# GpSimd fills the padding rows of batches 1 to 3, batch 1 is split in three pieces, batch 0's values are projected earlier

## What is computed

```python
q, k, v = heads(xn @ Wq + bq), heads(xn @ Wk + bk), heads(xn @ Wv + bv)      # xn = layernorm(x), 16 heads of 8
y  = softmax(causal(q @ k.T * scale)) @ v
qc, kc, vc = heads(xn @ Wcq + bcq), heads(ctx @ Wck + bck), heads(ctx @ Wcv + bcv)
y += softmax(qc @ kc.T * scale) @ vc
x = x + tanh(g_xattn[0]) * (y @ Wp + bp)
x = x + tanh(g_ffn[0]) * moe0(layernorm(x))      # top 2 of 8 experts, with a capacity
x = x + tanh(g_xattn[1]) * attention1(layernorm(x), ctx)      # one head
x = x + tanh(g_ffn[1]) * moe1(layernorm(x))      # top 2 of 8 experts
```

## Time and profile before

| | us |
|---|---|
| median of 3 runs | 383.36 (382.57 to 384.79) |
| the profiled execution: its own time | 384.66 |
| its span in the profile | 382.9 |
| busy PE, DVE, ACT, POOL | 331.7, 240.0, 188.9, 103.8 |
| mean granted TensorE clock | 0.957 of full speed |

### The profile page before, as it was taken

The page is one execution under the profiler, slowest core; times in us unless marked ns, Lnnn a source line. Parts: engine busy times, 40 slices in busy tenths (PEclk is TensorE's granted clock), DMA queues, the critical chain, the costliest instruction groups (busy, mean ns, idle before and its releaser), DMA issues.

```text
span 382.9 us, 6988 instructions
## 1 busy us (share of the span) xinstructions
PE 331.7 (87%) x2646; PEld 192.9 (50%) x2646; DVE 240.0 (63%) x566; ACT 188.9 (49%) x387; POOL 103.8 (27%) x173
## 2 busy tenths in 40 slices
PE   4879959988899998778979699999988499899994
PEld 2445624434343343333456467776775346575663
DVE  5787778888988888747545042233310958658765
ACT  3366237787778778667518622232217333324220
POOL 5526102125222322223276102223432201100000
PEclk9989968999999999999989879999999889999999
DMA  7779993121305002250061380000002100000100
GB/s 171 189 185 211 210 217 69 31 102 42 114 2 169 4 2 79 90 169 2 2 197 52 89 216 25 16 9 20 21 14 84 41 2 1 0 2 0 30 0 27
DMA packets 35635, 27.80 MB, mean 73 GB/s; under 512 B 5436, under 2 KB 32880, under 8 KB 35602
## 3 DMA queue, kind: packets, MB, share of 16 engines
q1 hardware_dynamic: 33718, 25.34, 26.4%
q0 software_dynamic: 1280, 1.88, 1.5%
q10 hardware_dynamic: 604, 0.14, 0.2%
HBM read 11.89 MB, written 5.26 MB: 45 GB/s over the span
## 4 chain that ended last, share of the span: by engine, by line
PE 70%; DVE 11%; ACT 6%; DMA 5%; issue 4%; POOL 2%; ACTq 1%; SPq 1%; POOLq 0%; DVEq 0%
PE psum L1433 11%; PE psum L1632 11%; PE psum L1663 7%; PE psum L1616 6%; PE psum L1651 4%; PE psum L1375 4%; PE psum L1399 4%; PE psum L1367 3%; PE psum L1451 2%; DVE nmax L1008 2%; PE psum L1311 2%; ACT ot_sb L787 2%; PE psum L1377 1%; PE psum L1564 1%; ACT qk L812 1%
## 5 line engine op out<-in xcount | busy, mean ns | idle before, releaser
L1008 DVE TENSOR_REDUCE nmax<-psum 128x2 f32<-128x1024 f32 (+2 forms) x88 | 104.5, 1216 | 21.2 <-PE psum L1375 12.8
L812 ACT ACTIVATE parts<-psum 128x512 f32<-128x512 f32 (+1 forms) x88 | 44.7, 569 | 12.9 <-PE psum L1399 12.3
L1151 DVE TENSOR_TENSOR qcat<-psum,qk_r 128x320 f32<-128x320 f32 x32 | 15.7, 491 | 45.9 <-ACT qk_r L853 45.8
L1632 PE MATMUL psum<-p_more,kcat 128*128 128x320 f32 x128 | 43.0, 478 | 0.7 <-DVE p_more L1142 0.7
L853 ACT ACTIVATE qk_r<-psum 128x320 f32<-128x320 f32 x32 | 14.0, 438 | 49.4 <-PE psum L1632 49.4
L709 POOL DMA_INDIRECT rows_back<-qcat,back_at x24 | 22.9, 954 | 56.1 <-ACT qcat L844 51.2
L1632 PEld LDWEIGHTS psum<-p_more,kcat 128*128 128x128 f32 x128 | 23.6, 202 | 14.4 <-issue 6.0
L1663 PE MATMUL psum<-h_t,kcat 128*128 128x512 f32 x64 | 30.1, 596 | 0.7 <-ACT h_t L823 0.7
L1375 PE MATMUL psum<-kcat,qcat 64*128 64x512 bf16 x128 | 25.9, 401 | 5.4 <-DVE nmax L1008 4.9
L1399 PE MATMUL psum<-qcat,kcat 64*128 64x256 bf16 x256 | 25.7, 280 | 3.4 <-ACT p_more L812 1.4
L1433 PE MATMUL psum<-parts,v_aug 128*9 128x256 f32 (+1 forms) x352 | 28.3, 366 | 0.0
(11 more groups left out here) (216 smaller groups left out, 605.4 us busy)
## 6 DMA issues: line engine op xcount, KB each, us to landing
kcat<-parts SPq DMA_DIRECT2D x18, 192.0 KB, 5.4
qcat<-parts SPq DMA_DIRECT2D x24, 128.0 KB, 4.8
kcat<-ones_b SPq DMA_DIRECT2D x8, 192.0 KB, 5.1
kcat<-in_L_ffn_wi_gate_dram SPq DMA_DIRECT2D x6, 256.0 KB, 3.2
kcat<-in_L_ffn_wi_up_dram SPq DMA_DIRECT2D x6, 256.0 KB, 4.0
kcat<-in_L_ffn_wo_dram SPq DMA_DIRECT2D x6, 256.0 KB, 4.5
parts<-in_L_ffn_w_dram SPq DMA_DIRECT2D x3, 512.0 KB, 5.6
rows_in<-zeros SPq DMA_DIRECT2D x1, 1290.0 KB, 6.0
```

The lines of the kernel that those rows point to most:

```text
L812: act.activation(p_slots[u % NPT][:, 0:w], s2_bank(s2_place[u])[:, 0:w], ACT.Exp, scale=SCALE).then_inc(p_in, 1)
L1008: dve.tensor_reduce(dst[:, :, n * g:n * (g + 1)], src.rearrange("p (r q k) -> p r q k", r=PAR, q=n), AX.X, ALU.max, negate=True).then_inc( ...
L1151: dve.tensor_tensor(hh[:, e % 2, f, 0:SLOTS], bank(3 + 2 * (i % 2))[:, 0:SLOTS], sg[:, i % 2, 0:SLOTS], ALU.mult).then_inc(hh_in[0], 1)
L1632: ins = pe.matmul(bank(2 + 2 * (i % 2) + m)[:, 0:SLOTS], w_t[e][:, m, f * P:(f + 1) * P], xs_t[:, e % 2, :], start=True, stop=True)
```

## The change

The padding rows of batches 1 to 3 are no longer written by DMA. GpSimd fills the whole `qcat` of a batch with zeros and the whole `kcat` with ones (as 32-bit words that hold two bf16 ones) in `fill(b)`, before the parts are laid out over them. `fill(1)` stands behind the last `rstd_group` of the first normalisation, `fill(2)` behind GpSimd's constants, and `fill(3)` behind its subtractions. VectorE splits batch 1 in three pieces as q, k and ck come. The jobs `v` and `cv` of batch 0 move ahead of `q`, `k` and `ck` of batch 3; `N_FIRST` stays.

```diff
         N_FIRST = len(jobs) - 5
-        for b in range(B):
+        jobs[-3:-3] = [("v", 0), ("cv", 0)]
+        for b in range(1, B):
             jobs += [("v", b), ("cv", b)]
...
+        TWO_ONES = 1.0 + 0x3F80 / 2.0 ** 23
+        def pad_count(b):
+            return 16 * 4 if b == 0 else 2
...
             def lay_out_batch(b):
+                sp.wait_ge(pad_in[b], pad_count(b))
                 sp.wait_ge(parts_in, b + 1)
...
-            pad(1)
             lay_out_batch(1)
-            pad(2)
-            pad(3)
             lay_out_batch(2)
...
+            def fill(b):
+                pool.memset(qcat[:, b].rearrange("p g c -> p (g c)").bitcast(F32), 0.0).then_inc(pad_in[b], 1)
+                pool.memset(kcat[:, b].rearrange("p g c -> p (g c)").bitcast(F32), TWO_ONES).then_inc(pad_in[b], 1)
+            fill(1)
             const(pool.tensor_copy(ident_b[:, :], ident[:, :]))
...
             const(pool.memset(v_aug[:, :, :, HD:HA], 1.0))
+            fill(2)
             for b in range(SPLIT_DVE, B):
...
+            fill(3)
...
             for b in range(1, SPLIT_DVE):
-                dve.wait_ge(job_act, taken_count(job_at("ck", b)))
-                split(b, 0, XW, True)
+                for job, first, end in (("q", 0, QW), ("k", QW, QW + S), ("ck", QW + S, XW)):
+                    dve.wait_ge(job_act, taken_count(job_at(job, b)))
+                    split(b, first, end, job == "ck")
```

More of the change, by code:

```diff
@@ L493, in _ @@
             sp.wait_ge(zero_in, 2)
-            pad(0)
+            for r in (M_ROW, M_ROW + 1):
+                sp.dma_start(every(kcat, 0, r), ones_b[:, :]).then_inc(pad_in[0], 16)
+                sp.dma_start(every(qcat, 0, r), zeros[:, 0:QW // 2].bitcast(BF16)).then_inc(pad_in[0], 16)
             sp.wait_ge(early_in, 1)
@@ L544, in _ @@
                     if n % 2 == 0 and par == 0:
-                        sp.wait_ge(pad_in[n // 2], 16 * 4)
+                        sp.wait_ge(pad_in[n // 2], pad_count(n // 2))
                     sp.dma_start(dst[:, PP * (n % 2):PP * (n % 2 + 1), :],
@@ L1358, in pass1_unit @@
                     pe.wait_ge(cat_in[b], 16 * 2 * NPROD)
-                    pe.wait_ge(pad_in[b], 16 * 4)
+                    pe.wait_ge(pad_in[b], pad_count(b))
                 if kind == "late" and part == 0:
```

## The result

| | before | after |
|---|---|---|
| median, both on the same chip | 384.08 us (382.57 to 390.33, 4 runs) | 394.32 us (393.3 to 398.75, 4 runs) |
| the profiled execution: time, span | 384.66, 382.9 | 393.66, 391.9 |
| busy PE, DVE, ACT, POOL | 331.7, 240.0, 188.9, 103.8 | 335.1, 252.2, 188.9, 117.3 |
| mean granted TensorE clock | 0.957 | 0.940 |

The change makes the kernel slower: ratio 1.0281, 95% interval 1.0242 to 1.0321, which is 10.8 us on 384. I had forecast 388.8 us and at most 392. The sign and the place were right, the size was not.

What follows compares the result with a forecast made beforehand. It took the start of pass 2, behind batch 1's split and the maxima's DMAs, to bound the kernel. Terms +6.0, +2.0 and -2.7, with VectorE at +5.9 partly catching up, gave +5.4 on 383.36: 388.8 us, range 382.5 to 392.

Steps and rivals of the forecast that it cites:

- The bound and the path: Start of pass 2 at 52.59 us: a shift there goes through to the end of the kernel.
- Part 1, the DMAs that go: SyncE's queue before pass 2: the maxima land 3.1 us after issue, not 5.8; -2.7 us, bounds -2.9 and 0.
- Parts 2 and 3, the split and the fills: VectorE before pass 1: pieces save 1.6 us, fills cost 7.6; together +6.0 us, bounds +4.5 and +7.4.
- Part 4: Moved jobs make fill(3) meet the two casts of split_max before pass 2: +2.0 us, range 0 to 3.5.
- unit 2 on TensorE, which then stands from 24.5 to 32: Pass 1: unit 2 queues behind VectorE's later first reduction, with TensorE standing from 24.5 to 32 us.
- Rival (a): Fills in the split hold nobody up, only parts 1 and 2 remain: 379.4 us, down to 378; chance 0.20.
- I put it at 0: ScalarE's split_middle(3) waits for GpSimd with v and cv of batch 1 behind it: cost taken as 0.
- The sum at P: First matmul of pass 2 on TensorE: start at 57.9 us against 52.59, +5.3.
- (b): Fills hold VectorE less and fill(3) misses split_max; pass 1 some 2.5 us late: 383 to 384.5 us; chance 0.11.
- (c): The maxima's landing before pass 2 stays 5.8 us: +8.1, 391.5 us; chance 0.07.

Runs made afterwards that it cites:

- e3: The changed kernel with fill(3) moved between GpSimd's two subtractions of batch 2; ratio 1.0131 to the kernel before.
- e9: The kernel of e7 with GpSimd also waiting for its own semaphore before fill(3) and between its two memsets; one time, 389.63 us.
- e14: The changed kernel with the jobs v and cv of batch 0 back in their old place; ratio 1.0076 to the kernel before.
- e7: The changed kernel with seven unused products of 128x512 f32 filling TensorE's gap before unit 2; ratio 1.0143 to the kernel before.
- e11: The kernel before with only the jobs v and cv of batch 0 moved; ratio 1.0004 to the kernel before.
- e4: The changed kernel with all three fills moved beside VectorE's reductions from PSUM; ratio 1.0039 to the kernel before.
- e10: The kernel before with only the split of batch 1 in pieces; ratio 1.0011 to the kernel before.
- e12: The kernel before with batch 1 split in pieces, pad(1) behind batch 1's layout, pads 2 and 3 behind the second maxima; ratio 0.9910 to the kernel before.
- e5: The changed kernel with each memset of the fills cut into eight pieces at the same places; ratio 1.0152 to the kernel before.
- e1: The changed kernel without its fills, padding by DMA as before, split in pieces and moved jobs kept; ratio 1.0004 to the kernel before.
- e2: The changed kernel with only the fills, batch 1 split in one piece and jobs in old order; ratio 1.0255 to the kernel before.

## Why the prediction missed

**The bound and the path: right.** A later start of pass 2 went through to the end (+9.67 at P, +10.5 at the last score matmul, +9.0 in the span). The other kernels of the table that start pass 2 later than before end it later by the same and 0.1 to 1.2 us more.

**Part 1, the DMAs that go: right as far as it can be seen.** Forecast 3.1 us from issue to landing and a gain of 2.7; measured 3.3 from issue to the first matmul and a gain of 2.6. But that matmul no longer waits for the DMA, so the landing itself is only known to be 3.3 us or less. VectorE, which I had at +5.9, is at +10.5 and sets the rest.

**Parts 2 and 3, the split and the fills: right in kind, 1.0 us too high.** The memsets took 1.80 to 2.07 and 2.65 to 2.80 us against my 1.8 and 2.65. The casts and `tensor_scalar` were held and the subtractions not, by the mechanism of the earlier trace rows. Forecast +6.0 for unit 2, measured +5.0. The Trainium skill, page "SBUF — State Buffer", section "Who interferes with whom", has the loser wait for a whole instruction of the other engine; the trace agrees for the long casts of the split, the longest 2.50 us under a memset of 2.80. For the cast at 50.94 its sentence is too mild: that one waited through what remained of one instruction and through two more, and the measurement decides.

**Part 4, "I take 2.0, as one `qcat` memset": failed.** It was 4.25 us, beyond my bound of 3.5. That bound took the rest of one memset for each of two casts. In fact the first cast met the subtraction L659 in front of `fill(3)` and was then let through at neither of the two ends of instructions (51.4 and 53.2), so it stood for all three. e3 takes 4.96 us off M by moving this one fill, and e9 shows that a pause of 0.06 us in GpSimd's work lets the casts through. That they meet was foreseen, and by the right path (`ck` of batch 3 behind the moved jobs): GpSimd's last subtraction moved 3.4 us against `split_max` (from e14 to after: ended 2.9 before it, now 0.5 behind its start), forecast 2.9.

**"What queues behind it: ... unit 2 on TensorE, which then stands from 24.5 to 32": this was where the sum lacked a term.** I saw the gap and priced what waited, but not the clock behind it. It stayed at 1.2 GHz until 41 us. Up to `split_max` that took 3.0 us more than the low clock of the kernel before takes there. e7 shows it: unit 2 at the same time, full clock, M 4.65 us earlier. After the next stop, while `split_max` was held, the low clock came again, from 55 to 68 us, but the kernel before has it too after its own stop, from 50 to 60. The profile had told me. Rival (a) of the prediction even counts a low clock of "some 3 us" after the gap of 1.67 us, as a gain if it goes. I used the row in one direction only.

**"I put it at 0", for ScalarE: no run speaks against it.** `split_middle(2)`, which I had not looked at, now stands behind the copies of the moved jobs and comes at 37.73, 4.7 us later than in e14. But GpSimd is done with the subtraction that needs it at 41.67 and then waits 3.16 us for `ck` of batch 3, and ScalarE itself waits 0.79 us for TensorE behind it. So that delay costs nothing here. What the moved jobs cost once the fills are there (by e14 7.9 us in the ratios, 5.2 in the span, and by e11 nothing without them) goes through the two terms above, the cast and the clock.

The sum at P: forecast 57.9, measured 62.26. The difference of 4.4 is -1.0 (parts 2 and 3), +3.0 (clock), +2.25 (part 4) and +0.1 (from the DMA to the matmul). The median went up by 10.2, or 10.8 by the ratio, against 9.0 for the span of the profiled execution: its clock of 0.940 was the highest of the four (another had 0.940 too, with 393.3; the others 0.937 with 394.97 and 0.911 with 398.75).

**The rivals.** (a), fills that hold nobody up, is out. e4 nearly is that kernel, and even it isn't faster. (b) and (c) are out too: all three fills met casts or `tensor_scalar`, and the landing fell to 3.3 us or less. The clock is in none of them as a loss.

**Still open.** Why the 32-column cast is passed over at the ends of GpSimd's back-to-back instructions, and the casts of batch 1 are not: in `fill(1)` and `fill(2)` three of four memsets took 0.15 us or more longer than in `fill(3)`, as if they had waited for a cast, and in `fill(3)` none did. And what sets how long the low clock lasts, 3.4 us in one kernel and 34 in another, and whether it comes at all: behind the gap of 1.13 us in e10 and e12 it did not. The length of the gap alone does not set it: in the profiled execution of e11 it is 37 us behind the same gap of 1.67 us that has 3.4 us in the kernel before.

## What to carry to other kernels

Before work is moved onto GpSimd, lay its instructions over VectorE's timeline and look at every cast, copy and `tensor_scalar` that they cover. Put the fill beside reductions from PSUM or subtractions, and count a train of back-to-back GpSimd instructions as one, as the worst case. Where a change makes TensorE stand, add to the gap what its following work costs at the lower clock, from rows of the same products at both levels. And where a small DMA lands late behind large ones, first try another order of SyncE's queue: here that, with the split in pieces, gave 3.5 us, and the change with its clearing by GpSimd cost 10.8.

## What the runs showed of the hardware

- A waiting VectorE cast is not always served when a GpSimd instruction ends. It was held 4.86 us over the rest of a subtraction of 2.62 us and two memsets of 1.80 and 2.65 us that followed it without a pause (after), and 2.42 us over the rest of eight memsets of together 2.94 us (e5). With pauses of 0.06 us between GpSimd's instructions, two casts took 0.54 and 1.60 us (e9). Casts of 256 and 512 columns did get their turn between two memsets (after, e5).
- Around a gap of TensorE the granted clock was low for very different times, also while it worked without a pause: 3.4 us after a gap of 1.67 (before), 7 after 0.59 (e1), 14 from within the gap of 6.32 on (after), 7 likewise with 6.87 (e14), 34 after 1.95 (e2), and not at all after 1.13 (e10, e12).
- Close behind the layouts of batch 2, the maxima's two DMAs of 12 KB took 5.2 to 6.3 us from issue to first use, and TensorE waited for them (before, e1, e10). With more time behind the layouts the first use came after 3.0 to 3.3 us and TensorE waited for other things, so they took no longer than that.
